# Experts' scatter-additions ordered half by half, and layer 1's first row tiles normalised between the last outputs

## The reference

```
x = x + gnn0(layernorm(x))
x = x + ffn0(layernorm(x))     # 8 experts of 256 -> 512 -> 256, gelu; the 2 best of the gate are added up
x = x + gnn1(layernorm(x))
x = x + ffn1(layernorm(x))     # shared MLP and 4 experts
gnn(h) = sage(relu(sage(h)));  sage(h) = segment_mean(h[src], dst) @ Wl.T + b + h @ Wr.T
ffn0:  h = gelu(einsum('td,edh->teh', x, W1) + b1);  y = einsum('teh,ehd->ted', h, W2) + b2
       out = einsum('td with mask of top 2', y, mask)
```

## Time and profile before

| | |
|---|---|
| runs, device time | median 1181.79 us of 3 (1181.7 to 1183.42) |
| span of the profiled execution | 1182.9 us; the profile gives no other time for it |
| TensorE busy | 1135.1 us, 96% |
| VectorE, ScalarE, GpSimd busy | 48%, 31%, 14% |
| expert stage, from its first takings by VectorE to TensorE's first transposes of layer 1 | 474.8 to 674.8 us |
| additions L2907 | 56, the first at 476.10, the last at 669.99 |

### The profile page before, as it was taken

The page is one execution under the profiler, slowest core; times in us unless marked ns, Lnnn a source line. Parts: engine busy times, 40 slices in busy tenths (PEclk is TensorE's granted clock), DMA queues, the critical chain, the costliest instruction groups (busy, mean ns, idle before and its releaser), DMA issues. The chain is left out here.

```text
span 1182.9 us, 22185 instructions
## 1 busy us (share of the span) xinstructions
PE 1135.1 (96%) x8024; PEld 853.5 (72%) x8024; DVE 563.3 (48%) x1532; ACT 361.8 (31%) x697; POOL 168.6 (14%) x160
## 2 busy tenths in 40 slices
PE   5989999999999997999999699999999999999998
PEld 4667777776668886888888577555566688866765
DVE  8888888834447677111111363000044355248654
ACT  5764554422211102333333333100022201044333
POOL 3300000000000456444445300000000000001000
PEclk9999999999999998999999799999999999999999
DMA  6610000047532446456664521120066445135101
GB/s 194 211 44 13 25 25 12 25 127 180 160 102 91 134 131 186 67 116 145 121 151 76 124 89 45 49 83 32 17 160 186 136 131 162 58 98 179 44 22 42
DMA packets 134097, 118.16 MB, mean 100 GB/s; under 512 B 23030, under 2 KB 122105, under 8 KB 134016
## 3 DMA queue, kind: packets, MB, share of 16 engines
q1 hardware_dynamic: 103392, 77.67, 22.8%
q0 software_dynamic: 12448, 18.95, 8.1%
q10 hardware_dynamic: 18176, 20.45, 5.1%
HBM read 67.34 MB, written 49.29 MB: 99 GB/s over the span
## 5 line engine op out<-in xcount | busy, mean ns | idle before, releaser
L1364 PE MATMUL b_pa<-adj,l_parts 128*128 (+2 forms) x980 | 141.7, 296 | 0.4 <-ACT adj L1295 0.4
L1364 PEld LDWEIGHTS b_pa<-adj,l_parts 128*128 128x128 f16 x980 | 91.2, 97 | 29.5 <-issue 0.5
L2907 POOL DMA_INDIRECT x<-ring,l_row_i x56 | 87.4, 1561 | 113.1 <-DMA x<-ring,l_row_i 75.5
L2714 PE MATMUL l_sum<-l_parts,ring 128*128 128x256 f32 x448 | 101.6, 380 | 0.2 <-ACT ring L2811 0.2
L1605 DVE SCALAR_TENSOR_TENSOR l_parts<-dense,scale,l_parts 128x256 f16<-128x256 f32 x48 | 23.2, 483 | 158.2 <-ACT l_parts L1596 158.2
L1572 PE MATMUL dense<-room,ring 128*128 128x512 f32 x200 | 93.9, 593 | 0.2 <-ACT ring L1553 0.2
L2714 PEld LDWEIGHTS l_sum<-l_parts,ring 128*128 128x128 f32 x448 | 83.0, 190 | 10.9 <-ACT ring L2811 0.4
L2290 PE MATMUL l_sum<-l_parts,adj 128*128 128x256 f16 x735 | 82.9, 273 | 1.2 <-DVE rows L2018 1.2
L2290 PE MATMUL l1b_sum<-l_parts,adj 128*128 128x256 f16 x735 | 82.9, 273 | 0.9 <-DVE rows L2018 0.9
L2290 PEld LDWEIGHTS l_sum<-l_parts,adj 128*128 128x128 f16 x735 | 71.2, 98 | 10.7 <-issue 2.7
L2290 PEld LDWEIGHTS l1b_sum<-l_parts,adj 128*128 128x128 f16 x735 | 71.4, 98 | 10.4 <-issue 2.4
(11 more groups left out here) (471 smaller groups left out, 1879.5 us busy)
## 6 DMA issues: line engine op xcount, KB each, us to landing
ring<-sums_and_zt SPq DMA_DIRECT2D x50, 256.0 KB, 3.4
l_expert_xr<-slots_in SPq DMA_DIRECT2D x28, 257.0 KB
l_parts<-in_L_ffn_W SPq DMA_DIRECT2D x12, 512.0 KB, 5.2
pre<-room ACTq DMA_DIRECT2D x34, 128.0 KB, 2.1
sums_and_zt<-ring SPq DMA_DIRECT2D x10, 320.0 KB, 2.3
ring<-inv SPq DMA_DIRECT2D x50, 64.0 KB, 4.0
sums_and_zt<-room ACTq DMA_DIRECT2D x5, 640.0 KB, 3.6
adj<-xt SPq DMA_DIRECT2D x5, 640.0 KB, 4.5
```

The lines of the kernel that those rows point to most:

```text
L1364: ins = nc.tensor.matmul(pa[f][:, 0:size], parts[:, k, a, f * P:(f + 1) * P], adj[:, k, ds(r * BW, size)], start=k == 0 and a == 0, stop=k ...
L2714: ins = nc.tensor.matmul(to[t], h[:, n, t * P:(t + 1) * P], w2[:, u, n, :], start=i == 0, stop=i == HB - 1)
L2907: pool.indirect_dma_start(out=g["x1"], in_=y[:, half, t, :], in_offset=None, compute_op=ALU.add, out_offset=bass.IndirectOffsetOnAxis(ap=i ...
```

## The change

It splits the semaphore `added` in two, one for each half. An addition waits for the same half of the preceding tile instead of both. So that tiles of different experts never add at once, VectorE waits for all former additions (`added(...)`) ahead of the first tile of an expert: ahead of tiles 1 and 2, of expert 1's later tiles and of each expert from 2 on. Its loop over experts is unrolled. The last tile has buffers of its own in weights no longer used (`y_last`, `ids_last`), its additions wait for no others and count on a semaphore that outlives the block (`last_added`); SyncE waits for that in the next block, ahead of loading chunk 1. In the old block VectorE normalises four row tiles only, and takes the last tile's first half between their statistics and the root, its second half behind the root. The fifth row tile is normalised by VectorE at the start of the next block. ScalarE's second sum of squares writes to the weights' buffer `w1[1]` and no longer waits for the last product.

```diff
@@ Normalise.sync, Normalise.vector
+            if c == 1:
+                sp.wait_ge(self.g["last_added"], 16 * (ST // P))
...
-        dve.sem_inc(self.s["norm_done"], CT)
+        four = FIRST_ROWS[0][1]
+        dve.sem_inc(self.s["norm_done"], four)
+        fifth = self.first_rows[:, four:CT, :]
+        dve.wait_ge(self.g["fifth_row_in"], 16)
+        root_free(self.nc, self.ch, fifth, self.st, self.mv, self.rstd, self.tmp)
+        self.nc.vector.tensor_scalar(fifth[:, 0, :], fifth[:, 0, :], self.mv[:, 0, 0:1], self.rstd[:, 0:1],
+                                     ALU.subtract, ALU.mult).then_inc(self.s["norm_done"], 1)
@@ experts
+    def added(eng, count):
+        for t in range(NT):
+            eng.wait_ge(s[f"added{t}"], count)
+        if eng is not nc.sync:
+            eng.sem_inc(s["settled"], 1)
...
         for n, (t, count) in enumerate(FIRST_ROWS):
-            settled = sp.value_load(g["from"][0:1, n:n + 1], min_val=E0 + LAST_MOST - 3 + n, max_val=STMAX - 2 + n)
-            sp.wait_ge(s["added"], 16 * NT * settled)
-            work.load_first_rows(sp, g["x1"], t, count, s[f"first_rows{t}"])
-        sp.wait_ge(s["all_added"], 1)
+            settled = from_end(sp, len(FIRST_ROWS) - n)
+            landed = sp.snap(settled * 16)
+            added(sp, landed)
+            work.load_first_rows(sp, g["x1"], t, count, g["fifth_row_in"] if n else s["first_rows0"])
@@ experts.scalar
-        total = total_on(act)
-        act.wait_ge(s["y_mm"], NT * total)
-        nc.scalar.activation(work.squares, work.rows[:, 0:2 * w2_size], ACT.Square, accum_out=small[:, 0, 0:1]).then_inc(s["squared"], 1)
+        nc.scalar.activation(squares, work.rows[:, 0:2 * w2_size], ACT.Square, accum_out=small[:, 0, 0:1]).then_inc(s["squared"], 1)
@@ experts.vector
-        def expert(e, u):
-            tiles, at = tiles_on(dve, e)
-            end = dve.value_load(g["tiles"][0:1, 2, ds(e, 1)], min_val=1, max_val=STMAX)
+        def expert(e, at):
+            u = e % 2
+            end = end_on(dve, e) if e < E0 - 1 else from_end(dve, 1)
+            added(dve, dve.snap(at * 16))
             with dve.Fori(at, end) as j:
                 one_tile(j, u)
-            dve.wait_ge(s["y_done"], NT * (at + tiles + 1))
-            dve.sem_inc(s[f"w_free{u}"], 1)
+            if e < E0 - 1:
+                dve.wait_ge(s["y_done"], NT * (end + 1))
+                dve.sem_inc(s[f"w_free{u}"], 1)
+            return end
 
         dve.sem_inc(s["y_done"], NT)
         scattered(dve, [SETTLED + 1])
         one_tile(0, 0, whole)
+        added(dve, 16)
         one_tile(1, 1, whole1)
+        added(dve, 16 * 2)
         for j in range(2, EARLY):
             one_tile(j, 0)
...
-            later_tiles(dve, e, lambda j: one_tile(j, e))
+            later_tiles(dve, e, lambda j: one_tile(j, e), ahead=lambda start: added(dve, dve.snap(start * 16)) if e else None)
...
-        root_free(nc, ch, rows, st, mv, rstd, tmp, landed=landed)
-        for t in range(CT):
+        def last_half(t):
+            dve.wait_ge(s["y_mm"], last * NT + (t + 1))
+            nc.vector.tensor_tensor(y_last[:, t, :], halves[t], b2[:, (E0 - 1) % 2, :], ALU.add).then_inc(s["y_done"], 1)
+
+        dve.wait_ge(s["ids_ready"], last + 1)
+        nc.vector.tensor_tensor(ids_last, ids[:, ds(last, 1), :].rearrange("p a t -> p (a t)"), least[:, ds(last, 1), :].rearrange("p a t -> p (a t)"),
+                                ALU.max).then_inc(s["ids_now"], 1)
+        four = FIRST_ROWS[0][1]
+        dve.wait_ge(s["first_rows0"], 16)
+        root_free(nc, ch, rows[:, 0:four, :], st, mv, rstd, tmp, between=lambda: last_half(0))
+        last_half(1)
+        for t in range(four):
...
-        dve.wait_ge(s["first_normed"], CT)
+        dve.wait_ge(s["first_normed"], four)
@@ experts.gpsimd
         def add_rows(j, half):
             pool.wait_ge(s["ids_now"], j + 1)
-            if not isinstance(j, int) or j:
-                pool.wait_ge(s["added"], 16 * NT * j)
             for t in range(NT):
+                if not isinstance(j, int) or j:
+                    pool.wait_ge(s[f"added{t}"], 16 * j)
                 pool.wait_ge(s["y_done"], NT * j + NT + t + 1)
                 pool.sem_inc(s["adding"], 1)
...
-        pool.wait_ge(s["added"], 16 * NT * total)
-        pool.sem_inc(s["all_added"], 1)
+        pool.wait_ge(s["ids_now"], last + 1)
+        for t in range(NT):
+            pool.wait_ge(s["y_done"], last * NT + (NT + t + 1))
+            pool.sem_inc(s["adding"], 1)
+            add(y_last[:, t, :], ids_last[:, t:t + 1], g["last_added"])
```

More of the change, by code:

```diff
@@ L1642 @@
 FIRST_ROWS = ((0, 4), (4, CT - 4))
-assert len(FIRST_ROWS) < EARLY
+TAIL = 2
+assert len(FIRST_ROWS) <= TAIL < EARLY and TAIL < LAST_MOST
 FIRST_FINAL = ((LAST_MOST - 2) * ST, (LAST_MOST - 1) * ST)
@@ L2563, in vector @@
         ch.done(nc.vector.tensor_tensor(self.shift, self.moved, self.start, ALU.subtract))
-        for n in range(len(FIRST_ROWS)):
-            ch.mark(nc.vector.tensor_scalar(g["from"][:, n:n + 1], cnt[:, 2, E0 - 1:E0], float(n - len(FIRST_ROWS)), None, ALU.add))
+        for n in range(TAIL):
+            ch.mark(nc.vector.tensor_scalar(g["from"][:, n:n + 1], cnt[:, 2, E0 - 1:E0], float(n - TAIL), None, ALU.add))
         NT = ST // P
@@ L2599, in experts @@
     assert NT == 2
+    free = w2[:, 0, :, :].rearrange("p n d -> p (n d)")
+    y_last, ids_last = free[:, HB * D - NT * D:HB * D].rearrange("p (t d) -> p t d", t=NT), ids[:, 0, :]
+    squares = w1[1].rearrange("p k n -> p (k n)")
     whole, whole1, halves = [py[:, 0, :], py[:, 1, :]], [py1[:, 0, :], py1[:, 1, :]], [py[:, 0, :], py1[:, 0, :]]
     s = {n: pr.sem("e_" + n) for n in ("w_in0", "w_in1", "w_free0", "w_free1", "rows_in", "turned", "xt_ready", "h_mm",
-                                       "h_done", "y_mm", "y_done", "ids_ready", "ids_now", "adding", "added", "all_added", "first_in", "all1_set", "squared", "totalled", "rooted",
-                                       "first_chain", "first_normed") + tuple(f"first_rows{t}" for t, _ in FIRST_ROWS)}
+                                       "h_done", "y_mm", "y_done", "ids_ready", "ids_now", "adding", "settled", "added0", "added1", "first_in", "all1_set", "squared", "totalled", "rooted",
+                                       "first_chain", "first_normed") + ("first_rows0",)}
     LOADS = EXPERT_LOADS
@@ L2611, in tiles_on, with start_on, end_on, from_end @@
                 eng.value_load(g["tiles"][0:1, 1, ds(e, 1)], min_val=0, max_val=STMAX - 1))
+    def start_on(eng, e):
+        return eng.value_load(g["tiles"][0:1, 1, e:e + 1], min_val=e, max_val=STMAX - LAST_MOST - (E0 - 1 - e))
+    def end_on(eng, e):
+        return start_on(eng, e + 1) if e < E0 - 1 else total_on(eng)
+    def from_end(eng, n):
+        at = TAIL - n
+        return eng.value_load(g["from"][0:1, at:at + 1], min_val=E0 + LAST_MOST - 1 - n, max_val=STMAX - n)
     def later_range(eng, e, tiles):
@@ L2618, in later_range, with later_tiles @@
                 eng.value_load(g["tiles"][0:1, 2, 1:2], min_val=2, max_val=STMAX))
-    def later_tiles(eng, e, one_tile):
+    def later_tiles(eng, e, one_tile, ahead=None):
         tiles = eng.value_load(g["tiles"][0:1, 0, e:e + 1], min_val=1, max_val=ONE_MOST)
@@ L2625, in later_tiles @@
         with eng.If(tiles > EARLY_ROWS[e] // ST):
+            if ahead:
+                ahead(start)
             with eng.Fori(start, end) as j:
@@ L2880, in vector @@
             dve.sem_inc(s[f"w_free{e}"], 1)
-        with dve.Fori(1, E0 // 2) as k:
-            expert(k * 2, 0)
-            expert(k * 2 + 1, 1)
+        at = start_on(dve, 2)
+        for e in range(2, E0):
+            at = expert(e, at)
+        last = at
         ch, rows = Chain(dve, s["first_chain"]), work.first_rows
         st, mv, tmp, rstd = norm_space
-        def landed(t):
-            if t in dict(FIRST_ROWS):
-                dve.wait_ge(s[f"first_rows{t}"], 16)
-        root_free(nc, ch, rows, st, mv, rstd, tmp, landed=landed)
@@ L2897, in gpsimd, with add @@
     def gpsimd(pool):
         rows_stored(pool)
+        def add(rows, at, landed):
+            pool.indirect_dma_start(out=g["x1"], in_=rows, in_offset=None, compute_op=ALU.add,
+                                    out_offset=bass.IndirectOffsetOnAxis(ap=at, axis=0)).then_inc(landed, 16)
         def add_rows(j, half):
             pool.wait_ge(s["ids_now"], j + 1)
-            if not isinstance(j, int) or j:
-                pool.wait_ge(s["added"], 16 * NT * j)
             for t in range(NT):
+                if not isinstance(j, int) or j:
+                    pool.wait_ge(s[f"added{t}"], 16 * j)
@@ L2905, in add_rows @@
                 pool.wait_ge(s["y_done"], NT * j + NT + t + 1)
                 pool.sem_inc(s["adding"], 1)
-                pool.indirect_dma_start(out=g["x1"], in_=y[:, half, t, :], in_offset=None, compute_op=ALU.add,
```

(9 more changed lines are left out.)

## The result

| | kernel before | kernel changed |
|---|---|---|
| median of the runs | 1183.56 us (22 runs) | 1186.44 us (22 runs) |
| profiled span | 1182.9 us | 1185.2 us |

The ratio of the two is 1.0024, with a 95% interval of 1.0013 to 1.0035: 2.8 us slower (0.0024 x 1183.56), and 2.3 us by the spans. The forecast was 1185.8 us and slower, worked out from a median of 1181.8 for the kernel before, which is 1183.56 over these 22 runs.

The account below looks back on a forecast made before the run. TensorE was taken to set the expert stage's pace, with about 10 us idle at its end from the order of additions. 6.4 + 2.5 - 0.8 - 4.1 = +4.0 on 1181.8 gave 1185.8 us, range 1182.0 to 1189.5.

Parts of the forecast that it names:

- The stall at tile 1's taking: Stage start: VectorE waits for tile 0's additions, delaying TensorE's second product of tile 2; +6.4 us (6.2 to 6.9).
- The clock behind it: Behind the early stall: TensorE's clock falls to 1.2 GHz after idling; +2.5 us.
- The second wait: VectorE's wait for tile 1's additions before taking tile 2: costs nothing, under cover of 1.6 us.
- the other bound: Second wait, if the clock stays up: cover gone, up to 0.9 us comes in place of the 2.5.
- Same-half order in the stage: Inside the stage: additions waiting only for their own half never lag behind TensorE's 7.35 per tile; -0.8 us.
- The waits at the seven later changes of expert: Changes of expert, experts 1 to 7: VectorE's waits cost nothing, covered by 2.1 us or more.
- The end: Stage end to chunk 1's transposes: earlier row loads, last addition and chunk 1 load; -4.1 us (-3.2 to -5.2).
- Both ways of the end: To chunk 1's transposes: VectorE's chain from chunk 1's load and TensorE's own work, forecast to meet at 683.4.
- A: Rival: waits at the start are covered, only the end moves; -4.9 us, 1176.9 us, chance 0.08.
- B: Rival: stall there but clock costs only 0.5, end gives full 5.2; +0.9, about 1182.7 us, chance 0.22.
- C: Rival: waits at later changes of expert bite too, one microsecond at each of seven; +11, 1193 us, chance 0.05.

Follow-up runs that it names:

- The first experiment: Changed kernel with VectorE's waits for the additions of tiles 0 and 1 moved to GpSimd; ratio 0.9956 to the kernel before, median 1177.58 us.
- the last experiment: Changed kernel, both early waits on GpSimd, 5 dummy products before layer 1's transposes, last tile's second half taken within the root chain; ratio 0.9966.

## Why the prediction was right

Slower by 4.0 was forecast and 2.8 measured (2.56 by the path to chunk 1). Point by point, times set against the same instants:

1. *The stall at tile 1's taking* was 6.4, came out at 6.12 (482.72 - 477.00, plus the 0.40 by which this run came to the stage earlier). The landing took 4.0 where I had put 4.2; VectorE went on 0.15 behind it, as allowed, and TensorE 0.06 behind VectorE's taking (482.66). The first experiment shows the cause: with the wait on GpSimd the stall is gone. From the start of the addition to VectorE's next instruction it was 4.15 (477.68 to 481.83).
2. *The clock behind it*, forecast 2.5, was 2.56 (6.18 - 3.62), and the 12-product fill takes 2.55 away with the stall left in place. It was no detail: as large as the net result.
3. *The second wait costs nothing*, right, and for the reason given: it is covered because the first has already delayed TensorE. Tile 2 was taken 2.6 before it was wanted. With the first wait moved it costs 6.48. The filled kernel also bears on the other bound: with the clock up, tile 2 was taken by 487.60 (486.85 + 0.75) and TensorE came at 488.35, so even then the second wait was hidden, by 0.75. But there the fill itself had held the product before by 0.94. From the changed kernel's own rows, a tile without the slow clock would have been wanted at 490.07 (482.72 + 7.35), 0.08 behind 489.99: that bound was close.
4. *Same-half order in the stage*, -0.8: -0.79. Seven kernels with the new order have the same 175.86, and the one with the second wait alone has its slow clock in this stretch. But the reason that I gave, the order, isn't shown to be the whole of it. Five of the seven have the stall, which puts TensorE behind VectorE in any case. Of the four without it, two lose nothing and the two with the filled end, where nothing of this stretch was edited, have 175.97 and 176.38. In the last experiment VectorE takes tile 3 as late as in the kernel before, and TensorE waits for it:

```profile
491.53 0.75 DVE L2896 TENSOR_TENSOR ring<-l_sum,l_parts 128x256 f32<-128x256 f32 x2
...
492.41 3.72 PE L2751 MATMUL l_sum<-l_parts,ring 128*128 128x256 f32 x16 [0.26 <-DVE ring L2896]
```

That costs 0.52 with the new order, as much as the 0.51 that the new end with the old order loses (176.37). What differs beside the order is how long after tile 1's second product VectorE comes to its first taking: 4.60 and 4.72 in the two kernels that lose nothing, 5.10 and 5.11 with the filled ends, 5.11 in the kernel before, 4.87 with the old order and the new end. So the size came out, and how much of it is the order's stays open.
5. *The waits at the seven later changes of expert*, nothing: those 24 tiles took 23 x 7.35 and the last, shorter 6.91, within 0.1, which leaves no room for them. All kernels with the new order have these waits; one without them was not run.
6. *The end* is **the term that was mis-sized: 5.3 instead of 4.1**, just beyond my bound of 5.2. I had let tile 25's second addition land and the rows' load be issued 5.2 after the addition's start (between 3.8 and 6.6), and the rows land 5.3 later. Measured were 4.17 (659.37 to 663.54) and 3.91 (to 667.45), 2.4 sooner. VectorE couldn't use all of that, as it then waited 1.14 for the last tile's first half; 1.2 came through. From there on each step kept its size: the low parts end 11.91 after chunk 1's load is issued (11.89 before), TensorE starts 1.00 behind VectorE's last normalisation (674.34), and GpSimd's last instruction didn't hold the block, since it ended at 675.44, behind TensorE's start.

Both ways of the end were forecast to meet; VectorE's came last, by 0.56, and the two kernels with fills confirm that it sets the end. Of the rivals, A (waits covered) fell by the 6.0 of idle TensorE. B had the right end but the wrong clock: it put the clock at 0.5. C fell with the 7.35 spacing. The net result lay between the forecast and B because the end gave 1.2 more than I had taken. That the median of 1186.44 lies so near the forecast's 1185.8 is in part luck: the base was 1.8 higher than the one I had added to.

What I didn't see beforehand is how the end splits. Most of its gain is the order of the additions alone (3.3 to 4.0 of 5.3), which pays at the end in a place that this part of the diff doesn't touch.

## What to carry to other kernels

Put a wait for a landing on the engine that has nothing urgent queued behind it: the same wait cost 6 us and a slow clock on VectorE and nothing on GpSimd. Two waits that hide one another must be moved together, as removing either brings nothing. And price a TensorE pause of several microseconds with the slow product behind it, here 2.6 on top of 6.

## What the hardware showed beyond that

- GpSimd goes on later behind a landing than VectorE. In the changed kernel tile 0's second addition landed 4.0 after its start, and VectorE's next instruction came after 4.15 (477.68 to 481.83). In the first experiment it landed after 4.3, and GpSimd's next instruction came after 5.26 (476.98 to 482.24). Over the runs it is 0.1 to 0.2 behind the landing where VectorE waits (five runs), and 0.9 to 1.1 where GpSimd does (five runs). Landings vary too: with the first wait alone this one took 4.9.
- A product of 256 columns in f32 stands as two matmuls of 0.22 to 0.23 us, 0.44 to 0.45 together (11.06 / 25, 5.45 / 12).
- In the kernel with the end filled the clock fell at about 669.3, within a wait of 1.50, and TensorE was partly idle in the windows ahead of it (columns as above):

```profile
666.00:667.00 1.00, 0.46 (x3) 1.00 0.75 103
667.00:668.00 1.00, 0.67 (x6) 1.00 0.12 8
668.00:669.00 1.00, 0.40 (x4) 1.00 1.03 121
669.00:670.00 1.00, 0.10 (x1) 0.68 0.06 7
```

- In the last kernel it stayed up through the same stretch of its run (TensorE busy 0.18, 0.90, 0.00 and 0.60 in the windows from 667 to 671, the dense products at 3.62) and fell only at about 683, after a wait of 2.14 that had ended at 681.60. What decides between the two isn't settled here.
- The two indirect additions of a tile start 1.86 apart when both halves are ready (483.35, 485.21), and 2.21 apart at the last tile (671.62, 673.83), with 0.65 of issue in place of 0.30. There the second half was taken by 673.04, only 0.14 before the first addition ended (673.18). In the last experiment it was taken by 665.09, 0.63 before the end of the first, and the two start 1.86 apart again (664.16, 666.02).
